# Turning softmax probabilities by VectorE blocks and DMAs in place of TensorE transposes, in a two-layer kernel

## The reference, cut to what matters

```python
q = jnp.einsum('bsd,de->bse', hidden_states, wq).reshape(B, S, H, DQ)
kv = jnp.einsum('bsd,de->bse', hidden_states, wkv)
k = kv[..., :H * DN].reshape(B, S, H, DN)
v = kv[..., H * DN:H * (DN + DV)].reshape(B, S, H, DV)
scores = jnp.einsum('bqhd,bkhd->bhqk', q[..., :DN], k) * scale
scores = jnp.where(causal[None, None], scores, NEG_INF)
probs = jax.nn.softmax(scores, axis=-1)
attn = jnp.einsum('bhqk,bkhd->bqhd', probs, v).reshape(B, S, H * DV)
return jnp.einsum('bse,ed->bsd', attn, wo)
```

## Time and profile before

| | us |
|---|---|
| median of 3 runs | 1087.95 (1087.87 to 1088.72) |
| span of the profiled execution | 1086.1 |
| TensorE busy | 1081.5 |
| VectorE busy | 746.5 |
| ScalarE busy | 561.8 |
| GpSimd busy | 741.4 |

### The profile page before, as it was taken

How to read it: one execution, slowest core, us unless ns; L and a number is a source line. 1 busy time by engine, 2 the same in 40 slices (tenths; PEclk the granted TensorE clock), 3 DMA queues, 4 the chain that set the end, 5 groups by cost and what they waited for, 6 DMA issues and landing times.

```text
span 1086.1 us, 21396 instructions
## 1 busy us (share of the span) xinstructions
PE 1081.5 (100%) x6376; PEld 957.6 (88%) x6376; DVE 746.5 (69%) x1842; ACT 561.8 (52%) x1690; POOL 741.4 (68%) x1030
## 2 busy tenths in 40 slices
PE   9999999999999999999999999999999999999999
PEld 8888878998998898889888988898899889988987
DVE  7598965567767666776667666666667666676675
ACT  4445221134745555556556646654665466555663
POOL 4777567997938972977487648864795579379911
PEclk9999999999999999999999999999999999999999
DMA  5111342111200210111011101110111022001102
GB/s 174 40 59 41 105 137 68 57 37 40 79 20 20 79 40 21 40 60 39 20 59 40 39 19 59 40 39 19 60 48 49 0 60 73 25 16 57 45 1 78
DMA packets 23875, 54.39 MB, mean 50 GB/s; under 512 B 3424, under 2 KB 4000, under 8 KB 23648
## 3 DMA queue, kind: packets, MB, share of 16 engines
q1 hardware_dynamic: 23488, 52.84, 15.2%
q10 hardware_dynamic: 288, 0.52, 0.1%
HBM read 51.26 MB, written 2.10 MB: 49 GB/s over the span
## 4 chain that ended last, share of the span: by engine, by line
PE 96%; POOL 3%; DVE 1%; issue 0%; ACT 0%; POOLq 0%; DVEq 0%
PE banks L186 28%; PE banks L187 28%; PE banks L188 28%; PE banks L2074 4%; PE banks L2093 3%; PE banks L2065 3%; POOL acc L534 1%; PE banks L1315 1%; POOL form_lo L1639 0%; PE banks L1177 0%; DVE mixed L883 0%; PE banks L1365 0%; POOL form_hi L1637 0%; POOL tT_lo L540 0%; POOL wc_lo L488 0%
## 5 line engine op out<-in xcount | busy, mean ns | idle before, releaser
L1639 POOL TENSOR_TENSOR form_lo<-wqk_stage,form_hi 128x256 fp32r<-128x256 f32 x192 | 141.7, 738 | 16.0
L1693 POOL TENSOR_SCALAR vf_hi<-wvo_stage 128x512 fp32r<-128x512 f32 (+1 forms) x48 | 26.3, 547 | 168.3 <-PE banks L188 155.0
L1973 ACT ACTIVATE prob<-prob,top 128x128 f32<-128x128 f32 (+1 forms) x256 | 115.7, 460 | 15.9 <-DVE top L2002 15.7
L1979 ACT ACTIVATE prob<-prob,inv 128x128 f32<-128x128 f32 (+1 forms) x256 | 102.7, 451 | 38.5 <-DVE inv L2008 38.5
L2002 DVE CUSTOM_DVE_ANT_0 prob<-banks,mask 128x128 f32<-128x128 f32 (+1 forms) x256 | 81.3, 355 | 59.4 <-PE banks L188 46.4
L2020 DVE TENSOR_TENSOR acc<-acc,banks 128x512 f32<-128x512 f32 x129 | 86.8, 677 | 35.9 <-PE banks L188 35.7
L186 PE MATMUL banks<-tT_hi,form_hi 128*128 128x512 f32 x256 | 105.6, 412 | 0.0
L187 PE MATMUL banks<-tT_lo,form_hi 128*128 128x512 f32 x256 | 100.2, 391 | 0.0
L188 PE MATMUL banks<-tT_hi,form_lo 128*128 128x512 f32 x256 | 100.1, 391 | 0.0
L186 PE MATMUL banks<-wo_hi,oT_hi 128*128 128x512 f32 x240 | 95.9, 400 | 0.0
L188 PE MATMUL banks<-wo_hi,oT_lo 128*128 128x512 f32 x240 | 93.6, 390 | 0.0
(11 more groups left out here) (351 smaller groups left out, 3730.1 us busy)
## 6 DMA issues: line engine op xcount, KB each, us to landing
wqk_stage<-in_w_qk SPq DMA_DIRECT2D x32, 512.0 KB, 3.2
wvo_stage<-in_w_v SPq DMA_DIRECT2D x34, 256.0 KB, 2.7
wvo_stage<-in_w_o SPq DMA_DIRECT2D x32, 256.0 KB, 2.7
wd_stage<-in_w_down SPq DMA_DIRECT2D x22, 256.0 KB, 2.6
gu_stage<-in_w_gu SPq DMA_DIRECT2D x10, 512.0 KB, 3.3
out<-acc SPq DMA_DIRECT2D x7, 256.0 KB, 2.0
acc<-in_x SPq DMA_DIRECT2D x6, 256.0 KB, 6.5
tab<-in_w_comb SPq DMA_DIRECT2D x1, 1300.0 KB, 6.0
```

The source lines that it names most:

```text
L1639: nc.gpsimd.tensor_tensor(form_lo[:, part], src[:, :], as_f32(form_hi[:, part]), ALU.subtract).then_inc(form_ready, 1)
L1973: ins = nc.scalar.activation(pr, pr, ACT.Exp, bias=top[:, n % 2, r:r + 1], scale=-1.0, accum_out=total[:, n % 2, r:r + 1])
L1979: ins = nc.scalar.activation(pr, pr, ACT.Copy, scale=inv[:, n % 2, r:r + 1])
```

## The change

Pairs 6 to 15 of the first group, all of the middle groups and 0 to 9 of the last (116 of 128) are no longer transposed by TensorE. After R comes Z: VectorE transposes `prob` in 32x32 blocks into `probT`, SP writes that to a scratch in device memory, waits for it, and reads it back with four DMAs into `pT`, each into 32 partitions, in pieces of 96 elements, so that the blocks lie where the whole transpose has them. H(n), in slot n + 2: ScalarE rounds two thirds of `pT` to `pT_hi`, VectorE makes `pT_lo`; the last third is used as it is. O(n) moves to slot n + 2, behind that slot's second product, and E of an odd pair behind the third. The other 12 pairs keep the transposes, with U for what T had on ScalarE and VectorE. `prob`, `pT_hi` and `pT_lo` have one buffer each, `pT` has two. The fills are laid out anew; all W(0, t) now lie in slots 0 to 3. SP's loads stand in the lists as D (`load_vo`) and K (`load_qk`).

```diff
+FIRST_BOUNCED, LAST_BOUNCED = 6, 10
-def with_pairs(slots, first=False):
+def with_pairs(slots, by_pe):
...
     for p, fill in enumerate(slots):
-        older = [] if first and p == 0 else [p - 1]
-        late = [p - 2] if p % 2 and not (first and p == 1) else []
-        steps += [("S", p)] + [("E", n) for n in late] + [("T", n) for n in older] + [("X", p)]
-        steps += fill[:1] + [("R", p)] + fill[1:]
-        steps += [("O", n) for n in older]
+        turned = [p - 1] if p - 1 in by_pe else []
+        landed = [p - 2] if p - 2 not in by_pe else []
+        steps += [("S", p)]
+        if not landed and p % 2 and p > 1:
+            steps += [("E", p - 2)]
+        steps += [("T", n) for n in turned] + [("H", n) for n in landed]
+        if not landed:
+            steps += [("U", n) for n in turned]
+        steps += [("X", p)]
+        made = 0
+        for at, step in enumerate(fill):
+            steps.append(step)
+            made += step[0] in "PQW"
+            if at == 0:
+                steps += [("R", p)]
+            if at == 1 and p not in by_pe:
+                steps += [("Z", p)]
+            if step[0] in "PQW" and made == 2 and landed:
+                steps += [("O", p - 2)]
+            if step[0] in "PQW" and made == 3 and landed and p % 2:
+                steps += [("E", p - 2)]
+        if made < 3 and landed and p % 2:
+            steps += [("E", p - 2)]
+        if landed:
+            steps += [("U", n) for n in turned]
+        steps += [("O", n) for n in turned]
...
 MIDDLE_SLOTS = [
...
+    [("L", 0, P5), ("P", 0, P3), ("P", 1, P1), ("L", 0, P3), ("W", 0, 0), ("W", 0, 1)],
+    [("P", 1, P6), ("W", 0, 2), ("P", 1, P2), ("W", 0, 3)],
+    [("L", 1, P2), ("P", 1, P7), ("W", 0, 4), ("P", 1, P4), ("W", 0, 5)],
+    [("L", 1, P4), ("P", 1, P5), ("W", 0, 6), ("L", 1, P5), ("W", 0, 7), ("K", 3), ("D", 2), ("D", 3)],
     [("P", 1, P3), ("Q", 0, P1), ("L", 1, P3), ("Q", 0, P6)],
     [("Q", 0, P2), ("P", 2, P1), ("M", 0, P2), ("Q", 0, P7)]]
...
 OUTER_SLOTS = [
-    [("P", 2, P6), ("Q", 0, P4), ("P", 2, P2), ("M", 0, P4)],
-    [("L", 2, P2), ("P", 2, P7), ("P", 2, P4), ("W", 1, 0), ("L", 2, P4), ("Q", 0, P5)],
-    [("M", 0, P5), ("W", 1, 1), ("Q", 0, P3), ("P", 2, P5), ("M", 0, P3), ("Q", 1, P1)],
-    [("L", 2, P5), ("P", 2, P3), ("Q", 1, P6), ("W", 1, 2), ("L", 2, P3), ("Q", 1, P2)],
-    [("M", 1, P2), ("W", 1, 3), ("P", 3, P1), ("Q", 1, P7), ("P", 3, P6), ("W", 1, 4)],
-    [("P", 3, P2), ("Q", 1, P4), ("L", 3, P2), ("P", 3, P7), ("M", 1, P4), ("P", 3, P4), ("W", 1, 5), ("L", 3, P4),
-     ("Q", 1, P5)],
-    [("M", 1, P5), ("W", 1, 6), ("Q", 1, P3), ("M", 1, P3), ("P", 3, P5), ("W", 1, 7), ("L", 3, P5)],
-    [("P", 3, P3), ("P", 4, P1), ("L", 3, P3), ("P", 4, P6)],
-    [("P", 4, P2), ("L", 4, P2), ("P", 4, P7)],
-    [("P", 4, P4), ("L", 4, P4), ("P", 4, P5), ("W", 2, 0), ("W", 2, 1)]]
+    [("P", 2, P6), ("Q", 0, P4), ("P", 2, P2), ("M", 0, P4), ("D", 4), ("D", 5), ("K", 4)],
+    [("L", 2, P2), ("P", 2, P7), ("P", 2, P4), ("L", 2, P4), ("P", 2, P5), ("W", 1, 0)],
+    [("L", 2, P5), ("P", 2, P3), ("W", 1, 1), ("Q", 0, P5), ("L", 2, P3), ("Q", 1, P1)],
+    [("M", 0, P5), ("Q", 0, P3), ("P", 3, P1), ("M", 0, P3), ("Q", 1, P6), ("W", 1, 2)],
+    [("Q", 1, P2), ("P", 3, P6), ("M", 1, P2), ("Q", 1, P7), ("W", 1, 3), ("K", 5)],
+    [("P", 3, P2), ("Q", 1, P4), ("L", 3, P2), ("P", 3, P7), ("M", 1, P4), ("P", 3, P4), ("W", 1, 4), ("L", 3, P4)],
+    [("Q", 1, P5), ("W", 1, 5), ("P", 3, P5), ("M", 1, P5), ("Q", 1, P3), ("L", 3, P5)],
+    [("M", 1, P3), ("P", 3, P3), ("W", 1, 6), ("L", 3, P3), ("W", 1, 7), ("D", 6), ("D", 7)],
+    [("P", 4, P1), ("P", 4, P6), ("P", 4, P2)],
+    [("L", 4, P2), ("P", 4, P7), ("P", 4, P4), ("L", 4, P4), ("P", 4, P5)]]
...
+MIDDLE = [("D", 0), ("D", 1), ("K", 2)] + with_pairs(MIDDLE_SLOTS + OUTER_SLOTS, ())
...
+        def bounce_pair(g, steps, n):
...
+            sp.wait_ge(block_turned, turn + 1)
...
+                sp.wait_ge(bounce_in[n % 2], landings(g, n - 2))
+            sp.dma_start(bounce[n % 2], probT[:, :]).then_inc(bounce_out, 16)
+            sp.wait_ge(bounce_out, 16 * (turn + 1))
...
+            sp.wait_ge(o_done, g * PAIRS + n - 1)
+            side = P // BLOCKS
+            for c in range(BLOCKS):
+                sp.dma_start(
+                    pT[c * side:(c + 1) * side, n % 2].rearrange("j (a n) -> j a n", a=BLOCKS),
+                    bounce[n % 2][:, c * 3 * side:(c + 1) * 3 * side].rearrange("(a j) n -> j a n", a=BLOCKS),
+                ).then_inc(bounce_in[n % 2], 16)
...
+                elif kind == "H":
+                    act.wait_ge(bounce_in[n % 2], landings(g, n))
+                    act.wait_ge(o_done, g * PAIRS + n)
+                    nc.scalar.activation(by_block(pT_hi[:, :]), landed(n)[:, 0:2], ACT.Copy).then_inc(pT_hi_done, 1)
...
+                elif kind == "Z":
+                    dve.wait_ge(norm_done, g * PAIRS + n + 1)
+                    if n > FIRST_BOUNCED or steps is not FIRST:
+                        dve.wait_ge(bounce_out, 16 * bounces(g, n))
+                    nc.vector.transpose(probT[:, :], prob[:, :].rearrange("p (b c n) -> p c b n", b=3,
+                                                                          c=BLOCKS)).then_inc(block_turned, 1)
...
+                elif kind == "H":
+                    dve.wait_ge(pT_hi_done, g * PAIRS + n + 1)
+                    nc.vector.tensor_tensor(by_block(pT_lo[:, :]), landed(n)[:, 0:2], by_block(as_f32(pT_hi[:, :])),
+                                            ALU.subtract).then_inc(pT_ready, 1)
...
-                    ins = nc.tensor.matmul(banks[:, O, cols.start + P:cols.stop], v_full[:, b, d], p_full[:, n % 2],
+                    ins = nc.tensor.matmul(banks[:, O, cols.start + P:cols.stop], v_full[:, b, d], second_keys(n),
                                            start=False, stop=True)
```

More of the change, by code:

```diff
@@ L143, in turns @@
     else:
-        before = [("P", 0, P7), ("W", 0, 0), ("W", 0, 1)]
+        before = [("P", 0, i) for i in (P1, P6, P7)]
     return len(before), before + [s for s in steps if s[0] in "PQW" and is_long(s) == long]
@@ L181 @@
 TOEP_AFTER = 6
+BLOCKS = 4
 def matmul3(nc, out, w_hi, w_lo, x_hi, x_lo, first, last):
@@ L1404, in attention @@
     acc, xT_hi, xT_lo, ident, _, banks, y_done = shared
-    w_qk, w_v, w_o, mask_dram, out = ins
+    w_qk, w_v, w_o, mask_dram, bounce, out = ins
     v_hi, v_lo, v_full, oT_hi, oT_lo, wo_hi, wo_lo, v_rest = late_sb
@@ L1408, in attention @@
      wvo_stage, mask) = lasting_sb
-    prob, p_full, pT_hi, pT_lo, top, total, inv, u3v = pair_sb
+    prob, probT, pT, pT_hi, pT_lo, top, total, inv, u3v = pair_sb
     HALF_G = GH * DH // 2
@@ L1446, in attention @@
     t_done = sem("t_done")
+    block_turned = sem("block_turned")
+    bounce_out = sem("bounce_out")
+    bounce_in = [sem(f"bounce_in{i}") for i in range(2)]
     pT_hi_done = sem("pT_hi_done")
@@ L1534, in turn_bank @@
         ring = LONG if long else SHORT
-        return banks[:, ring[(taken.index(step) - (len(taken) if steps is FIRST else own)) % len(ring)]]
+        at = taken.index(step) - (len(taken) if steps is FIRST else own) + (0 if long else SHORT_FROM)
+        return banks[:, ring[at % len(ring)]]
     def o_part(steps, n):
@@ L1556, in row_tiles, with bounces, landings, turned @@
     def row_tiles(p):
-        yield 0, prob[:, p % 2, 0:P], banks[:, S + p % 2, 0:P], mask[:, P:2 * P]
-        yield 1, prob[:, p % 2, P:3 * P], banks[:, S + p % 2, 2 * P:4 * P], mask[:, :]
+        yield 0, prob[:, 0:P], banks[:, S + p % 2, 0:P], mask[:, P:2 * P]
+        yield 1, prob[:, P:3 * P], banks[:, S + p % 2, 2 * P:4 * P], mask[:, :]
+    def bounces(g, n):
+        return g * PAIRS + n - FIRST_BOUNCED
+    def landings(g, n):
+        return 64 * (g * (PAIRS // 2) + (n - FIRST_BOUNCED) // 2 + 1)
+    def turned(steps, n):
+        return n + 1 if steps is FIRST else FIRST_BOUNCED + n - LAST_BOUNCED + 1
+    def by_block(ap):
+        return ap.rearrange("p (b a i) -> p b a i", a=BLOCKS, i=P // BLOCKS)
+    def landed(n):
+        return pT[:, n % 2].rearrange("p (a b i) -> p b a i", a=BLOCKS, b=3)
+    def second_keys(n):
+        return landed(n)[:, 2]
     def sync_program(sp):
@@ L1999, in group @@
                     dve.wait_ge(s_done, g * PAIRS + n + 1)
+                    if n and by_tensor(steps, n - 1):
+                        dve.wait_ge(t_done, turned(steps, n - 1))
+                    elif n or steps is not FIRST:
+                        dve.wait_ge(block_turned, bounces(g, n - 1) + 1)
                     dve.sem_inc(wait_passed, 1)
@@ L2062, in group @@
                         pe.wait_ge(moe_added, NT)
+                    if n >= 2 or steps is not FIRST:
+                        pe.wait_ge(s_top, g * PAIRS + n - 1)
                     keys = slice(b * SEQ, (b + 1) * SEQ)
@@ L2073, in group @@
                         part = slice(block * P, (block + 1) * P)
```

(4 more changed lines are left out.)

66 lines of the change are left out of this document (37 added, 29 removed).

## The result

The changed kernel takes 1186.63 us (median of four runs, 1184.37 to 1190.32) beside 1088.06 for the kernel before: 1.091 times as long, interval 1.089 to 1.093. It is slower by 98.6 us where 51 were predicted, and lies above the range of 1100 to 1170. The profiled execution has a span of 1186.1 us.

The account below looks back on a forecast made before the run. TensorE was taken as the bound, busy 1081.5 of 1086.1 us. The sum 1086.1 - 37.1 + 27.0 + 31.5 + 27.9 + 2.0 gave a span of 1137.4, a forecast time of 1139 us, range 1100 to 1170.

Parts of the forecast that it names:

- six places: Places (a) to (f) where TensorE would newly wait for other engines, 88.4 us together.
- The gain: Between slots on TensorE: removing the transposes saves 0.32 us for each of 116 pairs, 37.1 us.
- (a): Slot 7 of six middle groups: W1.0 waits 4.5 us for E5 behind P2.P5's combines and copies, 27.0 us.
- (b): Slot 12 of the first and six middle groups: S12 waits 1.6 us for L3.P4.
- (c): Slot 12 of the first and six middle groups: Q1.P3 waits 1.9 us for the bank of Q1.P5.
- (d): Slot 13 of the first and six middle groups: P3.P3 waits 1.0 us for L3.P5.
- (f): Last group: O10, directly behind O9, waits 2.0 us for E9 and U10, once.
- (e): Slot 15 into slot 0: waits before S0 and O14, 4.65 us at five loop-backs, 2.3 at two boundaries, 27.9 us.
- The clock falls in the new gaps: Rival: TensorE's idle gaps in slots 7 and five loop-backs lower its clock; eleven add 24 us, 1163 us; chance 0.17.
- The slow bounce: Rival: scratch round trip 2 us longer, O waits about 4 us a group in seven groups, 1167 us; chance 0.15.
- Faster: Rival: engines get through the chains of (a) and (e) early, most waits vanish; with none 1051 us; chance 0.10.
- half hidden: Rival: half of the waits hidden, 44 us left, 1095 us, slower by 7; chance 0.08.

Follow-up runs that it names:

- experiment 1: Kernel before, with only TensorE's transposes of the 116 pairs left out, order and copies unchanged: 1057.03 us, 0.971.
- Experiment 2: Changed kernel with unread matmuls filling the two long TensorE gaps, before W1.0 and before O14: 1169.84 us, 1.075 of the kernel before.
- experiment 12: Changed kernel with each pair's write to the scratch made twice, about 2 us more to land: 1235.18 us, 1.136 of the kernel before.
- best version: Changed kernel with E5, slots 11 and 12, O14, Z and W1.0 all reordered, and middle groups written out without the loop: 1101.05 us, 1.012.
- experiments 7: Changed kernel with O14 two products later in slot 0 of the middle groups and the last: 1181.95 us, 1.086 of the kernel before.
- 8: Changed kernel with E5, slots 11 and 12, O14, Z and W1.0 all reordered, loop kept: 1132.09 us, 1.040 of the kernel before.
- 10: Changed kernel with slots 11 and 12, O14 and Z reordered, E5 unmoved, W1.0 to W1.3 in slots 9 and 10, loop kept: 1141.12 us, 1.048.
- e5: Kernel before with its middle groups written out instead of the hardware loop: 1087.10 us, 0.9990 of the kernel before.
- e9: Changed kernel with all order repairs together and middle groups written out instead of the hardware loop: 1101.05 us, 1.012 of the kernel before.

## Why the prediction was wrong, and what held

**The direction and the places held.** Slower was given 0.88. Each of the six places is on the list, with the releaser named, and they hold 90 of its 97 us in the attention.

**The gain held**: 0.32 us a pair in the spacing of the matmuls (experiment 1 shows that alone it would have been partly given back to GpSimd).

**The waits** were 97.0 instead of 88.4, and 106.4 from matmul to matmul, which is how most of the prices had been worked out: 18.0 us short. Listed, (a) is 28.7 for 27.0, (b) 10.1 for 11.2, (c) 12.1 for 13.3, (d) 6.1 for 7.0 and (f) 2.5 for 2.0. (e) is 30.7 for 27.9: S0 waits 1.34 to 1.42 us in seven groups where I took 1.1, and O14 3.7 to 3.8 at the loop-backs (4.67 once) for 3.55, with 0.6 at the two boundaries for which I had 1.2. The 6.8 us elsewhere were priced at nothing; the places together are off by 1.8. The way round the loop took 3.0 to 3.4 us where I had 2.45. H's low part took 0.575 us on average, not 0.35. The transpose Z took 0.577, beside my 0.55.

**The step that failed** is a term that the sum left out, and it stands in the rivals: "The clock falls in the new gaps", 24 us, chance 0.17. I weighed it as another outcome *instead of* the forecast. It is what the forecast's own gaps of 3.5 to 4.5 us set off, and it was all but certain once these were on the list: each of the eleven had a stretch at 0.50 behind it. Experiment 2 takes the clock's fall away there and leaves the dependences, and 17 us go with it. Its size was about right, 26.6 us for 24, two of the thirteen stretches being behind gaps that I had not counted. The row that I used showed 7 matmuls a microsecond after an idle start and 11 four microseconds later, and that was a sign to price, not to set aside. By the rule of the Trainium skill's page "TensorE: Matmul & The Clock Gate" (section "Why this matters for your kernels"), which the prediction told and then set aside because no row showed it, the forecast would have been 1163; the trace agrees with the page for the eleven gaps of 3.7 to 4.8 us, and shows the same behind one of 2.5 and one of 1.8.

**The clock alone does not make up the miss.** The span came out 48.7 us above the forecast's 1137.4: 26.6 are the clock, 18.0 the waits, counted from matmul to matmul, and 4.1 stay without a place. With its 24 us of clock the forecast would have stood inside the range, and the time still above it.

**The range** followed from the same step. I took its ends from one rival at a time, so 1170 was the top. The upper bound of the waits was also added up wrongly: with (a) at 4.8, (e) at 30 and (b) to (d) at the stated half microsecond more each, they are 103 and not 97, and the forecast's upper end is 1154 and not 1148. With the clock that is 1178, which is 9 us below the measured time.

**The other rivals.** The slow bounce (0.15) did not occur: a landing takes 1.9 us for the write and 1.9 for the reads, of pieces of 384 bytes. The queue's 83520 additional packets took 2500 us of the 16 engines' time together (27.1% of the new span less 15.2% of the old), 0.03 us each, where the dear case had 0.11. What it would do was under-priced, 28 us for 2 us a pair against the 48.5 of experiment 12, which hold low clock too. *Faster* and *half hidden* have nothing for them.

**What stays open.** The best version has 13 us over the kernel before, and none here beats that. Its list adds to about 28 us in the attention (S8 1.7 to 2.3 us and S0 0.6 in seven groups, O's halves of a microsecond), and its clock is 0.994, some 7 us. How much of it is the price of O two slots on, and how much my order of the steps, I did not settle; no run keeps O two slots on and takes the waits before S8 away.

## What to carry to other kernels

Where an engine is full, removed work is worth its time only if the new order has no wait: write out for each next step who must have finished what, and do the same again for the step that takes its place, since experiments 7, 8 and 10 all moved a wait to a neighbour. A cover that a step had (a slot and two W steps for the loop's 2.5 to 3.4 us on VectorE) is part of its price, and it shows in no busy share. Where a forecast holds gaps of some 3 us and more on TensorE, the clock's fall belongs into the same sum and not among the alternatives; gaps of 1.7 to 2.7 us had it in under half of the cases here, which belongs into the range.

## What the runs showed of the hardware

**A gap costs more than itself.** In the changed kernel, gaps of 3.7 to 4.8 us brought the granted clock to 0.50 for 3.2 to 5.9 us of work, 1.6 to 2.9 us each on top. Taken over the traces of all fourteen kernels, with the idle time that the profile lists before a matmul of the attention: all 61 gaps of 2.8 us and more had a stretch at 0.50 that began in the gap or within 1.5 us behind it, 46 of 107 gaps of 1.7 to 2.7 us had one, and none of 132 gaps of 0.9 to 1.65 us had. In the middle band like gaps differ. In the best version two waits of S8 of 1.80 and 1.77 us, the first without a fall, the second with one (the columns as above):

```profile
616.00:618.00 2.00, 0.33 (x2) 1.00 0.96 276
618.00:620.00 2.00, 1.87 (x11) 1.00 0.83 286
```

```profile
720.00:722.00 2.00, 0.94 (x5) 1.00 0.89 226
722.00:724.00 2.00, 1.29 (x8) 0.92 0.88 264
724.00:726.00 2.00, 2.00 (x6) 0.50 0.43 161
```

**VectorE and GpSimd hold each other up.** H's low part has its block in SBUF now, not in a bank. Beside a working GpSimd and without one, in the changed kernel:

```profile
506.37 0.74 POOL L1720 TENSOR_TENSOR form_lo<-wqk_stage,form_hi 128x256 fp32r<-128x256 f32 x1
...
506.43 0.97 DVE L2123 TENSOR_TENSOR pT_lo<-pT,pT_hi 128x256 fp32r<-128x256 f32 x1
...
507.07 0.58 POOL L1718 TENSOR_SCALAR form_hi<-wqk_stage 128x256 fp32r<-128x256 f32 x1
...
512.58 0.42 DVE L2123 TENSOR_TENSOR pT_lo<-pT,pT_hi 128x256 fp32r<-128x256 f32 x1
```

It takes 0.42 us alone and 0.97 begun 0.06 us after GpSimd's 0.74, and GpSimd's next copy takes 0.58 where 0.40 is usual. In this trace 32 of the 116 low parts run while no GpSimd instruction does: 0.41 to 0.43 us. The other 84 take 0.63 on average, the longest 1.23 us. The page's mean over all is 575 ns; from a bank it took 419 ns. The Trainium skill's page "SBUF — State Buffer" (section "Who interferes with whom") says that a VectorE instruction with two inputs in SBUF contends with a GpSimd instruction that reads SBUF, as its second input comes through a read interface that the two share; the trace agrees. No run here takes this price apart from the rest.
